# A two-layer Fourier mixer on one core: softshrink shared by DVE and GpSimd, another prologue, and other orders of work around the MLP stage

## What is computed

```python
def softshrink(v, lam):                       # lam = 0.01
    return where(abs(v) > lam, v - sign(v) * lam, 0)

def afno_filter(x, w1, b1, w2, b2):           # 8 blocks of 16 channels
    xr, xi = real, imag of rfft2(x, axes=(1, 2), norm='ortho')
    o1r = relu(xr @ w1[0] - xi @ w1[1] + b1[0])
    o1i = relu(xi @ w1[0] + xr @ w1[1] + b1[1])
    o2r = softshrink(o1r @ w2[0] - o1i @ w2[1] + b2[0])
    o2i = softshrink(o1i @ w2[0] + o1r @ w2[1] + b2[1])
    return irfft2(o2r + 1j * o2i) + x

def layer(x, ...):
    h = afno_filter(layer_norm(x, n1_g, n1_b), w1, b1, w2, b2) + x
    g = layer_norm(h, n2_g, n2_b)
    return gelu(g @ mw1 + mb1) @ mw2 + mb2 + h    # 128 -> 512 -> 128
```

## Time and profile before

| | us |
|---|---|
| three runs | 1786.05, 1789.91, 1791.61 |
| median | 1789.91 |
| the profiled execution's own time | 1787.48 |
| its span, first to last instruction | 1785.7 |

### The profile page before, as it was taken

One profiled execution on the slowest core, in us unless ns is written; L12 is line 12 of the kernel. 1 busy time (PEld: TensorE's weight loads), 2 busy tenths in 40 slices (PEclk: granted clock), 3 DMA queues, 4 the chain that ended last, 5 costly groups with the idle time before them and its releaser, 6 DMA issues.

```text
span 1785.7 us, 35087 instructions
## 1 busy us (share of the span) xinstructions
PE 1636.1 (92%) x11184; PEld 1453.6 (81%) x11184; DVE 1195.5 (67%) x2880; ACT 934.6 (52%) x1778; POOL 630.5 (35%) x756
## 2 busy tenths in 40 slices
PE   0099989999999998999999998999999999899999
PEld 0088878888889887888889887888888988688888
DVE  7959956666646976666664895666664697566663
ACT  4335426666634534666652452666663453466665
POOL 4800004777750001677781000477775000111111
PEclk9999989999998998999998999999999999999999
DMA  8210061333320033333330006133332003211111
GB/s 246 100 54 1 1 220 59 101 105 105 100 80 1 1 115 117 103 103 106 106 101 24 1 1 220 54 97 103 106 107 84 1 1 126 77 36 31 34 36 48
DMA packets 164896, 138.85 MB, mean 78 GB/s; under 512 B 9186, under 2 KB 127332, under 8 KB 164804
## 3 DMA queue, kind: packets, MB, share of 16 engines
q1 hardware_dynamic: 164516, 137.15, 24.0%
q10 hardware_dynamic: 288, 0.46, 0.1%
HBM read 70.47 MB, written 67.11 MB: 77 GB/s over the span
## 4 chain that ended last, share of the span: by engine, by line
PE 44%; DVE 21%; POOL 17%; issue 15%; ACT 1%; DVEq 1%; DMA 1%; SPq 0%; POOLq 0%; ACTq 0%
PE ps L641 13%; PE ps L496 7%; PE ps L590 6%; POOL arena L1191 6%; POOL gz L1160 4%; DVE vsb L942 4%; POOL gz L1164 4%; PE ps L632 4%; PE ps L634 3%; PE ps L633 3%; DVE csb L944 3%; DVE usb L931 3%; DVE usb L932 2%; POOL arena L1198 2%; PE ps L621 2%
## 5 line engine op out<-in xcount | busy, mean ns | idle before, releaser
L641 PEld LDWEIGHTS ps<-mw,gel 128*128 128x128 f32 x4096 | 533.2, 191 | 43.3
L641 PE MATMUL ps<-mw,gel 128*128 128x128 f32 x4096 | 536.4, 274 | 0.0
L751 ACT ACTIVATE gel<-ps,mb1f 128x512 f32<-128x512 f32 x512 | 351.6, 687 | 269.9 <-PE ps L634 238.7
L1198 POOL TENSOR_TENSOR arena<-arena,mb2rep 128x512 f32<-128x512 f32 x128 | 163.5, 1277 | 886.0 <-ACT hn L737 886.0
L632 PE MATMUL ps<-hth,mw1h 128*128 128x512 f32 x512 | 262.9, 513 | 8.1 <-DVE htl L1024 7.8
L1191 POOL TENSOR_SCALAR arena<-xnext,rstd,shift 128x128 f32<-128x128 f32 x384 | 168.4, 457 | 217.7 <-DVE shift L1127 217.7
L737 ACT ACTIVATE hn<-arena,shift,rstd 128x128 f32 (+1 forms) x512 | 221.6, 482 | 35.6 <-DVE shift L1127 35.6
L1007 DVE TENSOR_TENSOR arena<-ps,arena 128x512 f32 (+1 forms) x64 | 44.2, 691 | 266.0 <-PE ps L613 241.9
L496 PE MATMUL ps<-cst,arena 128*128 128x128 f32 x1024 | 130.2, 294 | 90.3 <-DVE arena L904 81.4
L634 PE MATMUL ps<-hth,mw1l 128*128 128x512 f32 x512 | 204.4, 399 | 0.0
L496 PEld LDWEIGHTS ps<-cst,arena 128*128 128x128 f32 x1024 | 129.4, 208 | 90.8 <-DVE arena L904 81.5
(11 more groups left out here) (92 smaller groups left out, 2428.8 us busy)
## 6 DMA issues: line engine op xcount, KB each, us to landing
arena<-aside SPq DMA_DIRECT2D x128, 256.0 KB, 5.0
aside<-gz SPq DMA_DIRECT2D x96, 256.0 KB, 3.0
between<-xout SPq DMA_DIRECT2D x62, 256.0 KB, 2.3
xnext<-between SPq DMA_DIRECT2D x62, 256.0 KB, 3.0
out_dram<-xout SPq DMA_DIRECT2D x62, 256.0 KB, 2.3
aside<-first SPq DMA_DIRECT2D x32, 256.0 KB, 2.0
xnext<-in_x_dram SPq DMA_DIRECT2D x31, 256.0 KB, 3.0
mw1raw<-in_L_mw_dram SPq DMA_DIRECT2D x4, 256.0 KB, 2.5
```

The source lines that it names most:

```text
L641: mm = pe.matmul(ps[:, r % 2, P * i:P * i + P], gel[:, r % 2, m, P * i:P * i + P], mw2[:, m, :], start=(m == 0 and i == 0), stop=(m == CHU ...
L751: act.activation(gel[:, r % 2, m, :], ps[:, 2 + m % 2], ACT.Gelu, bias=mb1f[:, m:m + 1]).then_inc(gelu_out, 1)
L1198: pool.tensor_tensor(t, t, b, ALU.add).then_inc(mb2_done, 1)
```

## The change

- **Softshrink.** Two new constants per channel, `lower2` = -b2 - lam and `upper2` = -b2 + lam. DVE computes v = min(x, lower2) from PSUM and then max(v + 2 lam, x), reading PSUM a second time; both buffers now have the layout of the output (channel, frequency, part), so that PSUM is read with a step of 64 elements. POOL subtracts `upper2` and writes the arena and `yedge`. `v_out` now counts DVE's second operation and `y_done` POOL's; `edges_out` gets a semaphore of its own, `y_edge`.
- **Prologue.** Image 0 comes in five batches of (4, 8, 8, 8, 4) tiles, the first of them ahead of the parameters. The z tiles are shared: 15 to POOL, 15 to ACT, 2 to DVE. `build_spectral` is cut into parts and runs after the first batch's statistics. POOL makes the residual sums of 12 tiles and only after all z; DVE makes 20 of them (`R_DVE`) with temporary and gain in PSUM banks 6 and 7. In step 0 ACT alone takes all 32 `dft_w` groups out.
- **Before MLP.** `idft_w` of the first pair is split into groups 0 to 23 (`SOON`), done inside `idft_h` after group 25, and groups 24 to 31 after it, into banks 4 and 5; DVE adds them in two portions. `split_weights` runs inside `idft_h`. ACT takes groups 28 to 31 out alone.
- **After MLP.** POOL's last four tiles have another order: z rows first, then the two last biases, z rows, and gain products and sums at the end. DVE does x_new of tile 29 after the last statistics chain in place of before it. `build_spectral` of layer 1 runs between the evictions of step 2's `dft_w`, and `dc_bias` follows `dft_w`.

```diff
-PRO_ACT = (7, 6, 6, 3)
+BATCH = (4, 8, 8, 8, 4)
+PRO_POOL = (2, 4, 4, 4, 1)
+PRO_ACT = (2, 4, 4, 4, 1)
 CONSTS = 7 * P + 2 * BLOCKS
 EVEN = KWS + 1
 PB = 8
-R_DVE = 8
+R_DVE = 20
+PARTS = 12
 EARLY = 13
+SOON = 24
+V_DVE = SOON // 2 + 2
+V_ACT = CGROUPS - V_DVE
 R_POOL0 = TILES - R_DVE
-Z_DVE0 = TILES - sum(PRO_ACT)
+ROW0_BATCH = 2
+Z_DVE0 = TILES - sum(PRO_ACT) - sum(PRO_POOL)
...
+            turns = sorted(range(TILES), key=lambda t: 2 * t + 1 if t < R_POOL0 else t - R_POOL0)
+            for t in turns:
                 if t < R_POOL0:
...
                         store(TILES // 4 - 1, r)
+                    for r in range(4):
                         put_aside(s, TILES // 4 - 1, r)
...
+            def first_pair(s, a, b):
+
+                if a == 0:
+                    pe.wait_ge(h2_done, TILES * s)
+                for cg in (b - 2, b - 1):
+                    turned(s, cg)
+                t = slice(GROUP // 2 * a, GROUP // 2 * b)
+                for bank, m, h0 in ((6, DE, 0), (7, DO, H - ROWS)):
+                    dst = ps[:, bank - (2 if a else 0), 0:ROWS * GROUP * (b - a)]
+                    mm = pe.matmul(dst, m, v_of(s)[:, t, h0:h0 + ROWS, :], start=True, stop=True)
+                mm.then_inc(iw_soon if a == 0 else iw_mm, 1)
+
...
+                    if cg == SOON + 1:
+                        first_pair(s, 0, SOON)
...
-                if s % IMAGES == 0:
+                if s == 0:
+                    dc_bias(0)
+                dft_w(s)
+                if s and s % IMAGES == 0:
                     dc_bias(s // IMAGES)
-                dft_w(s)
...
-                        for r in (0, 2):
+                        for r in ((0, 2) if s else range(4)):
...
+            def build_done():
+
+                b2 = b2rep[:, :, :, :].rearrange("p q r c -> p q c r")
+                own.add(dve.tensor_scalar(lower2[:, :, :, :], b2, -1.0, -LAM, ALU.mult, ALU.add))
+                own.settle()
+                own.add(dve.tensor_scalar(upper2[:, :, :, :], lower2[:, :, :, :], 2 * LAM, None, ALU.add))
                 own.settle()
                 dve.nop().then_inc(spec_built, 1)
+
+            def scale_spectral(n):
+
...
+                    build_spectral(0)
+                if b == 1:
+                    scale_spectral(0)
+                for t in range(t0 + PRO_POOL[b], t0 + BATCH[b] - PRO_ACT[b]):
...
-                own.add(dve.tensor_tensor(by_row(gz0[:, :, :]), ztile(0, ROWS * t), gains(gain1[:, :]), ALU.mult))
+                tmp = ps[:, 6].rearrange("p (h c) -> p h c", h=ROWS)
+                own.add(dve.tensor_tensor(by_row(tmp), ztile(0, ROWS * t), gains(ps[:, 7, C:2 * C]), ALU.mult))
                 own.settle()
-                dve.tensor_tensor(first[:, h, :], first[:, h, :], gz0[:, :, :], ALU.add).then_inc(r_dve, 1)
+                dve.tensor_tensor(first[:, h, :], first[:, h, :], tmp, ALU.add).then_inc(r_dve, 1)
...
-                bias = b2rep[:, q].rearrange("p r c -> p (r c)").unsqueeze(1).to_broadcast([P, kws, P])
-                v = vsb[:, q].rearrange("p j r c -> p j (r c)")[:, 0:kws]
-                cl = csb[:, q].rearrange("p j r c -> p j (r c)")[:, 0:kws]
-                src = ps[:, 4 + q, 0:P * kws].rearrange("p (j k) -> p j k", j=kws)
-                dve.tensor_tensor(v, src, bias, ALU.add).then_inc(v_out, 1)
-                dve.wait_ge(v_out, UNITS * s + n + 1)
-                own.add(dve.tensor_scalar(cl, v, -LAM, LAM, ALU.max, ALU.min))
+                low = lower2[:, q].unsqueeze(2).to_broadcast([P, HALF, kws, 2])
+                v, cl = vsb[:, q, :, 0:kws], csb[:, q, :, 0:kws].rearrange("p c j r -> p c (j r)")
+                src = ps[:, 4 + q, 0:P * kws]
+                own.add(dve.tensor_tensor(v, src.rearrange("p (j r c) -> p c j r", j=kws, r=2), low, ALU.min))
+                if not (isinstance(n, int) and n < 2):
+                    dve.wait_ge(y_done, UNITS * s + n - 1)
                 own.settle()
-                v, cl = vsb[:, q], csb[:, q]
-                if kws == 1 or isinstance(b, int) and b == 0:
-                    edge = yedge[:, 0 if kws > 1 else 1, :, :, q]
-                    ins = dve.tensor_tensor(edge, v[:, 0], cl[:, 0], ALU.subtract)
-                    if kws == 1:
-                        ins.then_inc(y_done, 1)
-                        return
-                    own.add(ins)
-                    dst, v, cl = y_of(s)[:, q, :, 2:2 * GROUP], v[:, 1:], cl[:, 1:]
-                else:
-                    dst = y_of(s)[:, q, :, bass.ds(2 * GROUP * b, 2 * GROUP)]
-                dst = dst.rearrange("p c k -> p k c")
-                v, cl = (t.rearrange("p j r c -> p (j r) c") for t in (v, cl))
-                dve.tensor_tensor(dst, v, cl, ALU.subtract).then_inc(y_done, 1)
+                dve.scalar_tensor_tensor(cl, v.rearrange("p c j r -> p c (j r)"), 2 * LAM,
+                                         src.rearrange("p (m c) -> p c m", c=HALF), ALU.add, ALU.max).then_inc(v_out, 1)
...
+                    dve.wait_ge(spec_in, SPEC_IN * (s // IMAGES + 1))
+                    for cg in range(1, CGROUPS, 2):
+                        a_out(s, 2 * cg // CGROUPS, cg % (CGROUPS // 2) // 4, cg % 4)
+                        if cg // 2 < PARTS:
+                            build_part(cg // 2)
+                        if cg // 2 == PARTS:
+                            build_done()
+                    scale_spectral(s // IMAGES)
...
+                with dve.Fori(0, SOON // 4) as j:
                     for r in (1, 3):
                         v_out_(s, 4 * j + r, r)
+                split_weights(s)
+                dve.wait_ge(resid_in[0], RESID_IN[0] * (s + 1))
+                v_out_(s, SOON + 1, 1)
+                dve.wait_ge(iw_soon, s + 1)
+                h2_evens(s, 0, SOON)
+                v_out_(s, SOON + 3, 3)
+                own.settle()
+                h2_odds(s, 0, SOON)
+                own.settle()
...
+                        if known:
+                            h2(s, i, h)
+                        else:
+                            dve.wait_ge(iw_mm, PAIRS * s + 1)
+                            h2_evens(s, SOON, CGROUPS)
+                            own.settle()
+                            h2_odds(s, SOON, CGROUPS)
+                            own.settle()
+                            dve.nop().then_inc(h2_done, 2)
...
-                    if known >= 3:
+                    if 3 <= known <= PAIRS or last and known > PAIRS:
                         x_new(s, i + (2 * h - 5) // 4, (2 * h - 5) % 4)
...
+                    if known > PAIRS and not last:
+                        x_new(s, i + (2 * h - 5) // 4, (2 * h - 5) % 4)
...
-                split_weights(s)
...
+                pool.wait_ge(st_pro, b + 1)
+                for t in range(sum(BATCH[:b]), sum(BATCH[:b]) + PRO_POOL[b]):
+                    for i in range(ROWS):
+                        h = t * ROWS + i
+                        ins = pool.tensor_scalar(zrow(0, h), pairs(first[:, h, :]), prs[:, h:h + 1], pnm[:, h:h + 1],
+                                                 ALU.mult, ALU.add)
+                    ins.then_inc(z_pool, 1)
             pool.wait_ge(gain_in, 16)
-            done = [0, 0]
+            pool.wait_ge(z_pool, sum(PRO_POOL))
+            pool.wait_ge(z_act, sum(PRO_ACT))
+            pool.wait_ge(z_dve, Z_DVE0)
...
+                pool.wait_ge(gz_done, R_POOL0 + TILES * s)
+                for n in range(UNITS):
+                    q, kws = n % 2, 1 if n in (2, 3) else GROUP
+                    pool.wait_ge(v_out, UNITS * s + n + 1)
+                    cl = csb[:, q, :, 0:kws]
+                    high = upper2[:, q].unsqueeze(2).to_broadcast([P, HALF, kws, 2])
+                    if n < 4:
+                        edge = yedge[:, 0 if n < 2 else 1, :, :, q].rearrange("p r c -> p c r")
+                        ins = pool.tensor_tensor(edge, cl[:, :, 0], high[:, :, 0], ALU.subtract)
+                        cl, high = cl[:, :, 1:], high[:, :, 1:]
+                    if n not in (2, 3):
+                        k = 2 * GROUP * (spectrum_of(n) // 2)
+                        dst = y_of(s)[:, q, :, k + 2 * (n < 2):k + 2 * GROUP].rearrange("p c (j r) -> p c j r", r=2)
+                        ins = pool.tensor_tensor(dst, cl, high, ALU.subtract)
+                    ins.then_inc(y_done, 1)
...
+                for n in range(TILES):
+                    j, r = n // 4 - 1, n % 4
+                    if j >= 0 and not last:
+                        ready(j, r)
+                        z_rows(j, r)
+                        scaled(j, r)
+                    if n >= 2:
+                        biased(n - 2)
+                    if j >= 0 and not last:
+                        added(j, r)
+                j = TILES // 4 - 1
+                if not last:
+                    ready(j, 0)
+                    z_rows(j, 0)
+                    z_rows(j, 1)
+                for n in (TILES - 2, TILES - 1):
```

(31 more changed lines are left out.)

216 lines of the change are left out of this document (115 added, 101 removed).

## The result

| us | before | changed kernel |
|---|---|---|
| median (range) | 1788.14 (1786.05 to 1791.61, 4 runs) | 1702.16 (1697.58 to 1704.80, 4 runs) |
| ratio | | 0.9515, 95% interval 0.9487 to 0.9543 |
| the profiled execution, its span | 1787.48, 1785.7 | 1697.58, 1695.8 |

What follows compares the result with a forecast made beforehand. It took DVE to bound the filter, DVE behind POOL the prologue, and PE the MLP body. Softshrink 32, prologue 38.4 and 0.5, front of MLP 5, after MLP 19: 95 us off 1789.9 gives 1695, range 1680 to 1718.

Steps and rivals of the forecast that it cites:

- Rival 2: In the prologue, POOL's z rows hold DVE up as its additions did: about 20 us lost, 1715; 8%.
- PE's 2.53 us: In the filter stage, PE's work per unit between two `dft_h` blocks; the unit was forecast at 2.57 us.
- the edges: In the filter stage, DVE's wait for POOL's fourth unit before `edges`: 0.5 us per step off the softshrink gain.
- Rivals 1 and 4: Filter: DVE's minimum and maximum take 1.06 us each, 1709, 12%; POOL's subtraction and DVE exclude each other, 1781, 3%.
- The bound for a unit of 2.70: In the filter stage, the lower bound of the softshrink gain, put at 18 us in place of 32.
- Rival 3: Step boundaries and MLP's front: DVE's chain is late and the clock falls anyway; 12 us of gain go, 1707; 10%.
- rival 5: In the filter, PE idles between first units and the clock may fall: 2 to 5 us per stretch; no chance given.

## Why the prediction held, point by point

- **Prologue, 38.4 forecast, 37.0 measured.** Mechanism and order of ends as forecast (POOL's z rows last). DVE ends its fourth chain at 45.7, 1.2 us later than summed; part of that is what I had counted at nothing: beside POOL's z rows some products take up to 0.41 in place of 0.19. Rival 2 is out. That what follows `dft_w` is covered was the condition that carried the gain: 31.8 us to the filter in both kernels.
- **Softshrink, 32 forecast, 22.4 measured by its own run.** The mechanism holds, the size does not, and the failed step is "PE's 2.53 us": PE's own work is 2.65, since part of the weight load's wait was hidden behind `mix1`. The count was too high as well. With 0.19 the same sum would give 0.19 x 128 = 24, less 2 for the edges, 22; but in before only some 21 intervals per step were longer than 2.65 (0.18 x 21 = 3.8), and the end of the stage gives 1 us more. That is 4.8 per step, 98.3 -> 93.4, 19 in all where the clock plays no part, and that 22 is also what the run measured is chance. Rivals 1 and 4 are out: 684 and 687 ns, and a unit of 2.65 with `combine` (one operand in PSUM) at 0.42 and 0.41 beside POOL's subtraction. (The bound for a unit of 2.70 should read 16, not 18, with the edges taken off as elsewhere; nothing else depends on it.)
- **Front of MLP, 5 forecast, 0 to 4 measured.** The statistics came 32.9 us after `idft_h` starts, as forecast (33), and the first `gelu` 1.3 us earlier than without this part, but this does not arrive whole at the end.
- **After MLP, 19 forecast, 17.3 in the profile.** The waits before `dft_w` gave 15.2 us, `dft_w` of steps 1 and 3 2.2 and 2.9, and that of step 2 took 3.0 back. What is left of the last column, 21.7 - 15.2 = 6.5, is the front of MLP together with the clock in that stage (31 us at the lower level in place of 39, some 4 us by half of the difference, an estimate). The order alone is worth 18 us. Rival 3 is out. One term was much too small: the block copies beside POOL, priced 1.5 with no sum behind it, cost 3 to 4 us by the times. I had taken 0.35 per copy from the earlier trace rows, where z rows and short waits stood between POOL's additions; in the new place nothing does.
- **Margin.** I had put POOL's last z rows at 508 and PE's last `fc2` at 509.6, 1.6 us apart; they lie 1.3 apart (463.8 and 465.1). POOL's two biases back to back held one DVE instruction for 2.62 us.
- **Clock.** The forecast counted 2.3 us for each boundary. `dft_w` of steps 1 and 3 is 2.2 and 2.9 us shorter. The sum did not count that the stretches inside before's filter (4.5 us each, 102.8 against 98.3 in step 3) might go as well; rival 5 had only named them as possible. None is in the three profiles of the changed kernel, but the change does not rule them out: with the late block copies three filters have 3.4 us each at the lower clock (95.0 to 95.9 us in place of 93.4), and with softshrink undone one has 6.8. Why they come is open.

So the right total rests in part on luck. In the two profiled executions the kernel gained 90 us where 95 was forecast. Softshrink gave 12.6 less than forecast, the prologue with what follows 1.9 less and the part after MLP 1.7 less; the stretches at the lower clock in before's filter, which the sum did not have, gave 9.8, and the front of MLP, with the clock there, 1.5 more than forecast. By the medians the total is 7 us above the forecast; the profiled execution has 34 us at the lower clock where the two later profiles of the same kernel, at 1701.74 and 1702.81 us, have 51.

## What to carry to other kernels

To find the work of PE in a stretch, read the matmul rows, not the weight-load rows: a wait of the load counts only as far as the matmuls behind it run dry. When a wait is taken out of one engine's stream, look who used to get in during that wait. An early start of a stage is worth what the stages behind it can take, so sum the work of the helper that is moved and see where it now ends.

## What was not expected of the hardware

- A DVE instruction with two operands in SBUF can be held for several POOL instructions in a row: 6.12 us for two small copies, over five of POOL's two-input instructions without a wait. With a wait before every addition the same pair took 2.54. The Trainium skill (SBUF — State Buffer, Who interferes with whom) tells of the lock for one instruction; that the next ones in POOL's queue can take it again is what these rows add. It does not always. In before DVE got in between two POOL instructions that followed each other with no idle time (timeline of POOL; the earlier trace rows has the DVE instruction, 505.47 to 506.67):

```profile
505.38 1.26 POOL L1198 TENSOR_TENSOR arena<-arena,mb2rep 128x512 f32<-128x512 f32 x1
506.60 1.27 POOL L1164 TENSOR_TENSOR gz<-xnext,gz 128x512 f32<-128x512 f32 x1
```

  In all traces of this case DVE got in at such a boundary whenever POOL had last been idle before the instruction that ended there or the one ahead of it, and was held over the boundary when POOL had run eight or more instructions since; nothing in between occurs, and what decides is not shown.
- A DVE tensor_scalar on 8 elements per partition, with one operand only (455.59 above), was held for 2.62 us in the same way.
- POOL's one-input z rows (0.45 us each) hold DVE only little: 0.41 in place of 0.19 for the slowest product of the chain.
- POOL's subtraction, with its scattered write, is faster (1.10) than its additions (1.28).
